# VectorE's order in the head, and the clearing of a table and the comparison of indices spread over three iterations

## The chip, the cores and the metric

The kernel runs on one core of a Trainium2 chip. The metric is the device time of one execution in microseconds; lower is better. The engines are named TensorE (PE in rows; PEld is its loading of weights), VectorE (DVE), ScalarE (ACT), GpSimd (POOL) and SyncE (SP, which issues most DMAs).

## The reference, cut to what matters

Attention with four query heads for each key head, a residual and a layer norm; then a mixture of experts whose weights are a common matrix plus sparse entries, again with a residual and a layer norm. `x` is 8 x 512 x 512, there are 16 query heads and 4 key heads of 128, 8 experts, and 4096 sparse entries for each expert.

```python
q, k, v = x @ wq, x @ wk, x @ wv            # 16 heads of q, 4 of k and v, each 128 wide
out = softmax(mask(q k^T * 128**-0.5)) v    # causal, in chunks
x = layernorm(x + out @ wo)
logits = clip(xt @ gate_w.T, -50, 50); top_w, top_idx = top_k(logits, 2)
deltas = softmax(expert_atom_weights) @ atoms            # 8 x 4096
weighted = deltas * sigmoid(importance)
rows, cols = mask_idx // H, mask_idx % H                 # 4096 places, with repeats
contrib = segment_sum((xt[:, cols] * vals).T, rows)      # vals: the two chosen experts' entries
x = layernorm(x + xt @ W.T + contrib.T)
```

## The kernel before, in words

All engines have a program of their own, written out by hand; the order of the calls in each program is the order of its work, and semaphores join them. The attention is one loop over 32 iterations `it`, eight batches `b` of four groups `g`; an iteration takes one key head and its four query heads over 512 positions. Every fp32 matrix product is made of three passes over a high and a low part of each operand (lines 1532 to 1534): ScalarE or GpSimd rounds the high part (`kT_hi`, `qT_hi`, `pT_hi`, `oT_hi`, `w_hi`), VectorE or GpSimd subtracts it (`kT_lo`, `qT_lo`, `pT_lo`, `oT_lo`, `w_lo`). Inside an iteration, `n` counts heads: `scores`, then `maxima` on VectorE (line 1922), `exps` on ScalarE, `inverse` on VectorE (`row_inv`, line 1930), `normalize` on GpSimd (`probs`, line 1409), `transposes` on TensorE (line 1559), then `pT_hi` and `pT_lo` (line 1933), then `values_first` and `values_second` on TensorE. `values_second` waits for the last `pT_lo` of the iteration, the second query projection of the next iteration waits for `kT_lo`.

**The head** stands ahead of iteration 0. Besides the first projections and scores VectorE makes there the values of the sparse entries: `importance_shares` (two steps, lines 1001 and 1002) and `make_entries` (line 1035), which multiplies them by the mixture that TensorE makes in `mix_atoms` (line 947); and it splits the value weights (`wv_lo`, line 1978), which TensorE needs from iteration 0 on.

**Iterations 0 to 3** (batch 0, no routing yet) carry three further jobs:

- The table of expert weights in HBM is first written with the common matrix. It has 16 parts, in 8 pairs. GpSimd fills a part from `wT` (`fill_part`, line 898 and 1098), SyncE stores it (`store_part`, line 908), and the two buffers are used in turn, so that part k waits for the store of part k - 2 to land. `PART_PAIRS` says which pairs go with which iteration, and position in the tuple says the place in the iteration.
- Entries whose index occurs more than once have to be summed first, and written once. The 4096 indices lie as 32 columns of 128; a quad is four columns. For a quad `equal_indices` (line 1052) compares its indices with all in their column and gives 0/1 matrices `same`; `count_later` (line 1061, four instructions) counts for each entry the equal ones that come later; TensorE multiplies `same` with the entries (`sum_entries`, line 955), and VectorE copies the sums out (`keep_sums`, lines 1071 and 1072). The indices come by a broadcast load of half of them, `load_all_indices`.
- GpSimd splits `wo` (lines 1098, 1401) and the query and key weights of later iterations (lines 1098, 769), and SyncE stores these parts to be fetched by later batches.

Of the kernel before, what the change touches and what calls it, by code (L numbers as in the profile page):

```python
# [19 lines left out]
F32 = mybir.dt.float32  # L20
# [8 lines left out]
P = 128  # L29
# [8 lines left out]
QUAD = 4  # L38
# [3 lines left out]
PART_PAIRS = ((0, 1, 2), (3, 4, 5), (6, 7))  # L42
# [754 lines left out]
class Entries:  # L797


    def __init__(self, arena, zone, same, product, rows, sem):  # L800
# [22 lines left out]
        self.s_w_in, self.s_atoms_in, self.s_all_in = sem("w_ffn_loaded"), sem("atoms_loaded"), sem("idx_rows_loaded")  # L823
# [10 lines left out]
BANK_IMP, BANK_IDX, BANK_MIX = 0, 1, 2  # L834
SMALL_LINES, SMALL_MAX, SMALL_MIXTURE, SMALL_TURNED = 1, 2, 3, 4
# [75 lines left out]
def load_all_indices(sp, N, mask_idx, half):  # L911

    rows = mask_idx.unsqueeze(0).broadcast_to([P, NS])
    sp.dma_start(N.idx_all[:].rearrange("p j n -> p (j n)"), rows[:, half * NS // 2:(half + 1) * NS // 2]).then_inc(N.s_all_in, 16)
# [36 lines left out]
def sum_entries(pe, N, psum, bank, half):  # L951

    pe.wait_ge(N.s_same, (half + 1) * QUADS // 2)
    for j in range(NJ // 2):
        last = pe.matmul(psum[:, bank, j * 2 * NE:(j + 1) * 2 * NE], N.same[:, j // QUAD, j % QUAD],
                         N.parts[:, half * NJ // 2 + j].rearrange("p s e -> p (s e)"), start=True, stop=True)
    last.then_inc(N.s_sum, 1)
# [81 lines left out]
def split_entries(dve, N):  # L1039
    dve.wait_ge(N.s_entry, 1)  # L1040
    entry_step(dve, N, dve.tensor_copy(N.parts[:, :, 0], N.entry[:]))
    entry_step(dve, N, dve.tensor_tensor(N.parts[:, :, 1], N.entry[:], N.parts[:, :, 0].bitcast(F32), ALU.subtract))


def equal_indices(dve, N, q):
# [10 lines left out]
def count_later(dve, N, upper, q):  # L1056

    at = q % (QUADS // 2)
# [7 lines left out]
def keep_sums(dve, N, psum, bank, half, entry_sum):  # L1066

    dve.wait_ge(N.s_sum, half + 1)
    sums = psum[:, bank, 0:NJ * NE].rearrange("p (j s e) -> p j s e", s=2, e=NE)
    at = slice(half * NJ // 2, (half + 1) * NJ // 2)  # L1070
# [4 lines left out]
def entry_rows(dve, R, N, row_i):  # L1075
# [7 lines left out]
    dve.wait_ge(N.s_read, 2)  # L1083
# [53 lines left out]
def attention(nc, sem, s_passed, psum, ident, causal, upper, ones, R, F, E, N, table, row_i, entry_sum, y_acc, x_rows,  # L1137
# [62 lines left out]
    def sync(sp):  # L1200
# [53 lines left out]

        def slot(j, use, g):
# [26 lines left out]
        load_all_indices(sp, N, mask_idx, 0)  # L1282
        for j in range(3):
            keep_slot(j, 1)

        def iteration(b, g, it, kind, route, job):
# [13 lines left out]
            slot(3, it + 1, after)  # L1300
            if kind == "end":
# [10 lines left out]
            if not route and g < len(PART_PAIRS):  # L1312
                for k in PART_PAIRS[g][:1]:
                    store_part(sp, N, d_dram, 2 * k)
                    store_part(sp, N, d_dram, 2 * k + 1)
# [1175 lines left out]
```

## Time and profile before

| | |
|---|---|
| median of 3 runs | 1854.17 us (1852.67 to 1855.17) |
| profiled execution | 1852.85 us, its span 1851.1 us |
| TensorE busy | 1780.5 us, 96% of the span |
| VectorE / ScalarE / GpSimd busy | 67% / 44% / 43% |
| mean granted clock of TensorE | 0.989 of 2.4 GHz |
| the chain that ended last | TensorE 81%, VectorE 6%, issue 4%, GpSimd 3%, DMA 2% |

The profile is one execution. A matrix product's end is modelled, so its busy time is not its peak rate; what counts is where TensorE is idle and for whom. The windows give busy time by stretch, the waits who ended the idle time, and the timeline single instructions. Iteration 0 takes about 30 to 78 us, iteration 1 up to 128, iteration 2 up to 178, and batch 0 ends near 234 us.

### The profile page before, as it was taken

To read this page: it belongs to the slowest core of one execution; us is meant where nothing else is said; L and a number is where in the kernel's file an instruction comes from. 1 tells how busy PE (TensorE), PEld (TensorE's weight loads), DVE (VectorE), ACT (ScalarE), POOL (GpSimd) and SP (SyncE) were. 2 spreads that over 40 slices of the span, in tenths; PEclk is the share of its full clock that TensorE was granted. 3 is DMA by queue.
4 is the path that set the end of the run, shared out by engine and by line. 5 is a ranking of instruction groups with operands and counts; after the bars stand their busy time and mean duration, and the time that the engine had idled before them with its cause. 6 is when DMAs were issued, how large, how long until landed. Compare 5 with 4: busy or idle time off the path is not lost.

```text
span 1851.1 us, 33403 instructions
## 1 busy us (share of the span) xinstructions
PE 1780.5 (96%) x9290; PEld 1503.1 (81%) x9290; DVE 1243.4 (67%) x3879; ACT 814.4 (44%) x2059; POOL 801.1 (43%) x1092
## 2 busy tenths in 40 slices
PE   8999999999999999999999999999999999999992
PEld 6788888888888888888888888888888887777772
DVE  5467567775777577757776777677766777763266
ACT  4443444443444344534544544454444443333344
POOL 6675335445444333323332333233323334666563
PEclk9999999999999999999999999999999999999996
DMA  9556353334333444454544444454445338544698
GB/s 327 197 208 221 109 205 115 115 109 145 120 116 113 155 146 153 147 170 133 164 155 173 136 149 158 155 179 152 148 137 211 114 126 308 199 160 160 229 336 315
DMA packets 157103, 317.93 MB, mean 172 GB/s; under 512 B 23056, under 2 KB 66224, under 8 KB 146160
## 3 DMA queue, kind: packets, MB, share of 16 engines
q1 hardware_dynamic: 138624, 275.83, 43.8%
q0 software_dynamic: 18288, 39.80, 6.9%
q8 instruction: 89, 1.46, 0.3%
q14 instruction: 102, 0.84, 0.1%
HBM read 227.30 MB, written 88.28 MB: 170 GB/s over the span
## 4 chain that ended last, share of the span: by engine, by line
PE 81%; DVE 6%; issue 4%; POOL 3%; DMA 2%; ACT 2%; DVEq 1%; SPq 0%; another core or an unknown queue 0%; ACTq 0%; POOLq 0%
PE psum L1532 22%; PE psum L1534 22%; PE psum L1533 21%; PE psum L1559 7%; PE psum L2298 2%; PE psum L2300 2%; PE psum L2299 2%; DMA token_rows<-x,ids_now 1%; DVE pT_lo L1933 1%; PE psum L370 1%; ACT probs L1809 1%; PE psum L792 1%; POOL probs L1409 1%; POOL expert_weights L1429 1%; POOL expert_slots L647 0%
## 5 line engine op out<-in xcount | busy, mean ns | idle before, releaser
L1409 POOL TENSOR_SCALAR probs<-probs,row_inv 128x128 f32<-128x128 f32 (+3 forms) x512 | 307.3, 624 | 428.1 <-DVE row_inv L1930 426.0
L1809 ACT ACTIVATE probs<-probs,neg_max 128x512 f32<-128x512 f32 (+3 forms) x512 | 282.5, 554 | 360.4 <-DVE neg_max L1922 358.3
L1532 PE MATMUL psum<-xT_hi,w_hi 128*128 128x512 f32 x640 | 252.9, 395 | 1.9 <-DVE kT_lo L1933 1.2
L1534 PE MATMUL psum<-xT_hi,w_lo 128*128 128x512 f32 x640 | 250.3, 391 | 0.0
L1533 PE MATMUL psum<-xT_lo,w_hi 128*128 128x512 f32 x640 | 250.0, 391 | 0.0
L1922 DVE CUSTOM_DVE_ANT_0 probs<-psum,causal 128x512 f32<-128x512 f32 (+3 forms) x512 | 223.3, 488 | 35.0 <-PE psum L1534 14.7
L1933 DVE TENSOR_TENSOR pT_lo<-psum,pT_hi 128x512 fp32r<-128x512 f32 (+1 forms) x384 | 206.5, 594 | 23.3 <-ACT pT_hi L1819 23.1
L1819 ACT CAST pT_hi<-psum 128x512 fp32r<-128x512 f32 (+1 forms) x384 | 172.4, 526 | 68.3 <-PE psum L1559 68.2
L1532 PE MATMUL psum<-wo_hi,oT_hi 128*128 128x512 f32 x496 | 196.8, 397 | 0.0
L1534 PE MATMUL psum<-wo_hi,oT_lo 128*128 128x512 f32 x496 | 194.1, 391 | 0.0
L1533 PE MATMUL psum<-wo_lo,oT_hi 128*128 128x512 f32 x496 | 193.6, 390 | 0.0
L1532 PE MATMUL psum<-kT_hi,qT_hi 128*128 128x512 f32 (+3 forms) x512 | 173.5, 339 | 0.5 <-DVE qT_lo L1947 0.5
L1559 PEld LDWEIGHTS psum<-ident,probs 128*128 128x128 f32 x1280 | 145.7, 140 | 29.9 <-DVE pT_lo L1933 11.2
L1559 PE MATMUL psum<-ident,probs 128*128 128x128 f32 x1280 | 161.5, 273 | 7.1 <-DVE pT_lo L1933 3.6
L1533 PE MATMUL psum<-kT_lo,qT_hi 128*128 128x512 f32 (+3 forms) x512 | 165.7, 324 | 0.0
L1534 PE MATMUL psum<-kT_hi,qT_lo 128*128 128x512 f32 (+3 forms) x512 | 165.1, 322 | 0.0
L1387 POOL CAST v_hi<-v_raw 128x512 fp32r<-128x512 f32 x32 | 27.4, 855 | 300.3 <-PE psum L1534 284.8
L1947 DVE SCALAR_TENSOR_TENSOR qT_lo<-psum,qT_hi 128x512 fp32r<-128x512 f32 x128 | 88.4, 690 | 96.3 <-ACT qT_hi L1823 92.2
L1823 ACT ACTIVATE qT_hi<-psum 128x512 fp32r<-128x512 f32 x128 | 76.2, 595 | 165.5 <-PE psum L1534 164.2
L1532 PE MATMUL psum<-pT_hi,v_hi 128*128 128x512 f32 (+1 forms) x384 | 140.4, 366 | 5.0 <-DVE pT_lo L1933 4.5
L1532 PEld LDWEIGHTS psum<-xT_hi,w_hi 128*128 128x128 f32 x640 | 120.5, 188 | 26.0 <-DVE kT_lo L1933 1.6
L1534 PEld LDWEIGHTS psum<-xT_hi,w_lo 128*128 128x128 f32 x640 | 120.3, 188 | 25.5
(251 smaller groups left out, 3878.1 us busy)
## 6 DMA issues: line engine op xcount, KB each, us to landing
w_hi<-split_qk_weights SPq DMA_DIRECT2D x140, 256.0 KB, 2.7
w_lo<-split_qk_weights SPq DMA_DIRECT2D x140, 256.0 KB, 3.0
wo_hi<-split_out_weights SPq DMA_DIRECT2D x27, 1024.0 KB
wo_lo<-split_out_weights SPq DMA_DIRECT2D x27, 1024.0 KB
expert_weights_hi_lo<-split_expert_weights SPq DMA_DIRECT2D x8, 2048.0 KB, 9.6
x_in<-in_L_attn_x_dram SPq DMA_DIRECT2D x8, 1024.0 KB, 7.2
expert_weights<-fill SPq DMA_DIRECT2D x16, 512.0 KB, 4.0
attn_residual<-y_acc SPq DMA_DIRECT2D x8, 1024.0 KB
```

The lines of the kernel that those rows point to most:

```text
L1409: last = pool.tensor_scalar(p, p, row_inv[:, buf, i:i + 1], 1.0, ALU.mult, ALU.mult)
L1532: pe.matmul(dst, hi_s, hi_m, start=start, stop=False)
L1533: pe.matmul(dst, hi_s, lo_m, start=False, stop=False)
L1534: return pe.matmul(dst, lo_s, hi_m, start=False, stop=stop)
L1559: last = pe.transpose(psum[:, BANKS_PT[unit], at:at + P], probs[:, buf, src:src + P], ident[:])
L1809: last = act.activation(probs[:, buf, a:a + w], probs[:, buf, a:a + w], ACT.Exp, bias=neg_max[:, buf, i:i + 1], scale=-1.0, accum_out=row_ ...
L1819: act.copy(pT_hi[:, buf, a:z], psum[:, BANKS_PT[u], 0:z - a]).then_inc(s_pt_hi, 1)
L1823: act.mul(qT_hi[:, buf], psum[:, bank, :], SCALE).then_inc(s_q_hi, 1)
L1922: last = dve.tensor_tensor_reduce(probs[:, buf, a:a + w], psum[:, BANK_S + bank, col:col + w], causal[:, T - w:T], -1.0, -MASKED, ALU.add, ...
L1933: dve.tensor_tensor(lo, src, hi.bitcast(F32), ALU.subtract).then_inc(done, 1)
L1947: dve.scalar_tensor_tensor(out=qT_lo[:, buf], in0=psum[:, bank, :], scalar=SCALE, in1=qT_hi[:, buf].bitcast(F32), op0=ALU.mult, op1=ALU.su ...
L2298: pe.matmul(dst, hi_of(j, c), hi, start=c == 0, stop=False)
```

## The change

In the head VectorE leaves the importance shares until behind the first `inverse`, and `wv_lo` until behind the first maxima. The pairs of parts go 2, 3, 3 to iterations 0, 1, 2 where they went 3, 3, 2; the place at an iteration's tail, behind the last normalization, is gone, and there is a new first place behind weight slot 3. The eight quads go 2, 3, 3 to iterations 0, 1, 2 where they went 0, 4, 4; indices are loaded in four pieces of two quads into two halves of the buffer. The sums follow with each iteration.

```diff
-PART_PAIRS = ((0, 1, 2), (3, 4, 5), (6, 7))
+PART_PAIRS = ((None, 0, 1), (2, 3, 4), (5, 6, 7))
+QUADS_OF = ((0, 1), (2, 3, 4), (5, 6, 7))
+QUAD_BUFS, LOAD_QUADS = 4, 2
@@ sum_entries
+    pe.wait_ge(N.s_same, quads[-1] + 1)
+    pe.wait_ge(N.s_chain, PARTS_MADE)
+    for k, q in enumerate(quads):
@@ equal_indices
-    at = q % (QUADS // 2)
-    if at == 0:
-        dve.wait_ge(N.s_all_in, 16 * (q // (QUADS // 2) + 1))
-        if q:
-            dve.wait_ge(N.s_sum, 1)
+    at, k = q % QUAD_BUFS, q // LOAD_QUADS
+    if q % LOAD_QUADS == 0:
+        dve.wait_ge(N.s_all_in[k % 2], 16 * (k // 2 + 1))
+    if q >= QUAD_BUFS:
+        dve.wait_ge(N.s_sum, 1 + (q - QUAD_BUFS in QUADS_OF[1]))
@@ SyncE, iteration
             slot(3, it + 1, after)
+            if not route and g < len(PART_PAIRS):
+                store_pair(PART_PAIRS[g][0])
...
             if not route and g < len(PART_PAIRS):
-                for k in PART_PAIRS[g][1:]:
-                    store_part(sp, N, d_dram, 2 * k)
-                    store_part(sp, N, d_dram, 2 * k + 1)
-            if not route and g == 1:
-                sp.wait_ge(N.s_counted, QUADS // 2)
-                load_all_indices(sp, N, mask_idx, 1)
+                store_pair(PART_PAIRS[g][2])
+            if not route and g < 2:
+                sp.wait_ge(N.s_counted, LOAD_QUADS * (g + 1))
+                load_all_indices(sp, N, mask_idx, g + 2)
@@ GpSimd, iteration
             slot(3, it + 1)
+            if not route and g < len(PART_PAIRS):
+                fill_pair(PART_PAIRS[g][0])
...
             if kind != "end":
                 normalize(n + 4, 0)
-            if not route and g < len(PART_PAIRS):
-                for k in PART_PAIRS[g][2:]:
-                    fill_pair(k)
@@ TensorE, iteration
-            elif g >= 2:
-                pe.wait_ge(N.s_read, g - 1)
+            elif g:
+                pe.wait_ge(N.s_read, g)
...
-            if not route and kind == "group":
-                sum_entries(pe, N, psum, BANKS_PT[0], g - 1)
+            if not route and g < len(QUADS_OF):
+                sum_entries(pe, N, psum, BANKS_PT[0], QUADS_OF[g])
@@ VectorE, head
-        importance_shares(dve, N)
         kT(0)
         keep_mixture(dve, N, psum)
-        dve.wait_ge(F.s_wv_hi, 1)
-        dve.tensor_tensor(wv_lo[:], wo_raw[:, 0:C, :], wv_hi[:].bitcast(F32), ALU.subtract).then_inc(s_wv, 2)
         qT(0, 0, BANK_B)
         qT(1, 1, BANK_A)
         dve.wait_ge(N.s_const, 4)
         maxima(0, 0)
+        dve.wait_ge(F.s_wv_hi, 1)
+        dve.tensor_tensor(wv_lo[:], wo_raw[:, 0:C, :], wv_hi[:].bitcast(F32), ALU.subtract).then_inc(s_wv, 2)
         inverse(0, 0)
+        importance_shares(dve, N)
         make_entries(dve, N, psum, BANK_B)
@@ VectorE, iteration (first and second quad: before and behind the inverses, as before)
             route_logits(dve, R, tt, (6,), products)
-            if quad is not None:
-                equal_indices(dve, N, quad + 2)
+            for q in quads[2:3]:
+                equal_indices(dve, N, q)
...
-            if quad is not None:
-                equal_indices(dve, N, quad + 3)
+            for q in quads[2:3]:
+                count_later(dve, N, upper, q)
             if kind in ("group", "batch"):
                 kT(it + 1)
...
-            if quad is not None:
-                count_later(dve, N, upper, quad + 2)
             if kind != "end":
                 qT(n + 4, 0, bank_of_query(0, kind))
...
-            if quad is not None:
-                count_later(dve, N, upper, quad + 3)
```

The work of VectorE in the head, where `entry` are the values of the sparse entries. Before:

```order
L1017 TENSOR_SCALAR gap_f<-row_f,spare_f 128x32
L1001 TENSOR_SCALAR entry<-entry 128x256
L1002 RECIPROCAL entry<-entry 128x256
L1933 TENSOR_TENSOR kT_lo<-psum,kT_hi 128x512
L1025 COPY eawT<-psum 64x8 x2
L1978 TENSOR_TENSOR wv_lo<-wo_raw,wv_hi 128x2048
L1947 SCALAR_TENSOR_TENSOR qT_lo<-psum,qT_hi 128x512 x2
L1922 ISA probs,neg_max<-psum,causal 128x512
```

After the change (between the two pieces stand the rest of the four maxima):

```order
L1025 TENSOR_SCALAR gap_f<-row_f,spare_f 128x32
L1948 TENSOR_TENSOR kT_lo<-psum,kT_hi 128x512
L1033 COPY eawT<-psum 64x8 x2
L1962 SCALAR_TENSOR_TENSOR qT_lo<-psum,qT_hi 128x512 x2
L1937 ISA probs,neg_max<-psum,causal 128x512
...
L1937 ISA neg_max 128x1
L1996 TENSOR_TENSOR wv_lo<-wo_raw,wv_hi 128x2048
L1945 RECIPROCAL row_inv<-row_sum 128x4
L1009 TENSOR_SCALAR entry<-entry 128x256
L1010 RECIPROCAL entry<-entry 128x256
L1043 TENSOR_TENSOR entry<-psum,entry 128x128 x2
```

`kT_lo` and the two `qT_lo` moved ahead of `wv_lo` and the two steps on `entry`.

GpSimd from the tail of iteration 0 (`v_lo`, the normalization of the next iteration's first head) into iteration 1 (the second head's normalization, then weight slot 3). Before:

```order
L1392 TENSOR_TENSOR v_lo<-v_raw,v_hi 128x512
L1409 TENSOR_SCALAR probs<-probs,row_inv 128x128
...
L1409 TENSOR_SCALAR probs<-probs,row_inv 128x512
L1098 TENSOR_SCALAR fill<-wT 128x1024 x2
L1409 TENSOR_SCALAR probs<-probs,row_inv 128x128
...
L1409 TENSOR_SCALAR probs<-probs,row_inv 128x512
L1098 TENSOR_SCALAR w_hi<-w_raw 128x512
L769 TENSOR_TENSOR w_lo<-w_raw,w_hi 128x512
```

After:

```order
L1406 TENSOR_TENSOR v_lo<-v_raw,v_hi 128x512
L1423 TENSOR_SCALAR probs<-probs,row_inv 128x128
...
L1423 TENSOR_SCALAR probs<-probs,row_inv 128x512
L1423 TENSOR_SCALAR probs<-probs,row_inv 128x128
...
L1423 TENSOR_SCALAR probs<-probs,row_inv 128x512
L1108 TENSOR_SCALAR w_hi<-w_raw 128x512
L771 TENSOR_TENSOR w_lo<-w_raw,w_hi 128x512
L1108 TENSOR_SCALAR fill<-wT 128x1024 x2
```

The fill of a pair of parts moved from between the two normalizations to behind slot 3.

VectorE in iteration 1, from `oT_lo` to the last `pT_lo`; `same` is a comparison of a quad, `equal_later` one of its four counts, and a "..." stands for the counts left out and their second instructions. Before:

```order
L1933 TENSOR_TENSOR oT_lo<-psum,oT_hi 128x2x256
L1052 TENSOR_TENSOR same<-idx_all,idx_f 128x512
L1933 TENSOR_TENSOR oT_lo<-psum,oT_hi 128x2x256
L1052 TENSOR_TENSOR same<-idx_all,idx_f 128x512
L1933 TENSOR_TENSOR kT_lo<-psum,kT_hi 128x512
L1933 TENSOR_TENSOR pT_lo<-psum,pT_hi 128x512 x2
L1933 TENSOR_TENSOR pT_lo<-psum,pT_hi 128x256
L1061 ISA equal_later,dup<-same,upper 128x128
...
L1947 SCALAR_TENSOR_TENSOR qT_lo<-psum,qT_hi 128x512
L1061 ISA equal_later,dup<-same,upper 128x128
...
L1947 SCALAR_TENSOR_TENSOR qT_lo<-psum,qT_hi 128x512
L1933 TENSOR_TENSOR pT_lo<-psum,pT_hi 128x512 x2
```

After:

```order
L1948 TENSOR_TENSOR oT_lo<-psum,oT_hi 128x2x256
L1061 TENSOR_TENSOR same<-idx_all,idx_f 128x512
L1948 TENSOR_TENSOR oT_lo<-psum,oT_hi 128x2x256
L1070 ISA equal_later,dup<-same,upper 128x128
...
L1070 ISA dup 128x1
L1948 TENSOR_TENSOR kT_lo<-psum,kT_hi 128x512
L1948 TENSOR_TENSOR pT_lo<-psum,pT_hi 128x512 x2
L1948 TENSOR_TENSOR pT_lo<-psum,pT_hi 128x256
L1962 SCALAR_TENSOR_TENSOR qT_lo<-psum,qT_hi 128x512 x2
```

Two runs of four counts went from between `pT_lo`, `qT_lo` and `qT_lo`; one run stands now ahead of `kT_lo`.

## Rows read from the trace of the kernel before

**Rows 1.** Windows: busy PE, PEld, DVE, ACT, POOL; clock, DMA share, GB/s

```profile
77.00:125.00 48.00, 43.23 (x230) 36.74 (x229) 32.12 (x97) 18.87 (x52) 34.92 (x43) 1.00 0.61 214
125.00:172.00 47.00, 44.13 (x239) 38.01 (x238) 33.35 (x98) 19.27 (x53) 30.98 (x38) 0.98 0.58 212
```

**Rows 2.** TensorE's waits from 0 to 235 us: in total, times, longest

```profile
PE psum L1532 <- DVE pT_lo L1933: 4.5, 2, 2.9
PE psum L1559 <- POOL probs L1409: 3.2, 1, 3.2
PE psum L1532 <- DVE kT_lo L1933: 1.2, 1, 1.2
PE psum L1532 <- DVE qT_lo L1947: 0.5, 1, 0.5
```

**Rows 3.** Timeline, TensorE in the head: start us, us, instruction, idle before

```profile
19.91 0.50 PE L1532 MATMUL psum<-xT_hi,w_hi 128*128 128x512 f32 x1 [1.18 <-DVE kT_lo L1933]
```

**Rows 4.** Windows with the low granted clock (columns as in rows 1)

```profile
31.00:35.00 4.00, 4.00 (x16) 3.59 (x16) 2.07 (x11) 1.04 (x3) 3.42 (x6) 0.62 1.08 403
170.00:174.00 4.00, 4.00 (x12) 3.29 (x13) 2.21 (x9) 0.59 (x1) 0.00 (x0) 0.57 0.98 293
```

**Rows 5.** Timeline, ScalarE (first row) and VectorE in the head

```profile
15.68 0.59 ACT L1827 CAST kT_hi<-psum 128x512 fp32r<-128x512 f32 x1 [3.17 <-PE psum L1534]
...
16.69 0.66 DVE L1001 TENSOR_SCALAR entry<-entry 128x256 f32<-128x256 f32 x1
17.38 1.75 DVE L1002 RECIPROCAL entry<-entry 128x256 f32<-128x256 f32 x1
...
20.14 2.38 DVE L1978 TENSOR_TENSOR wv_lo<-wo_raw,wv_hi 128x2048 fp32r<-128x2048 f32 x1
...
27.77 0.18 DVE L1930 RECIPROCAL row_inv<-row_sum 128x4 f32<-128x4 f32 x1 [1.31 <-ACT probs L1809]
30.84 0.49 DVE L1035 TENSOR_TENSOR entry<-psum,entry 128x128 f32<-128x128 f32 x2 [2.90 <-PE psum L947]
```

**Rows 6.** Chain that ended last (first row), then timeline, 82 to 100 us

```profile
82.90 7.18 DMA expert_weights<-fill
...
84.27 0.17 DVE L1930 RECIPROCAL row_inv<-row_sum 128x4 f32<-128x4 f32 x1
...
91.26 2.06 POOL L1409 TENSOR_SCALAR probs<-probs,row_inv 128x128 f32<-128x128 f32 x4
...
99.65 2.27 POOL L1409 TENSOR_SCALAR probs<-probs,row_inv 128x128 f32<-128x128 f32 x4 [4.28 <-DVE row_inv L1930]
```

**Rows 7.** Timeline, iteration 1: VectorE's comparisons beside GpSimd's splitting of weights

```profile
109.27 0.68 DVE L1052 TENSOR_TENSOR same<-idx_all,idx_f 128x512 fp32r<-128x512 int32 x1
...
112.67 1.29 POOL L1401 TENSOR_TENSOR wo_lo<-wo_raw,wo_hi 128x512 fp32r<-128x512 f32 x1 [0.18 <-POOL wo_hi L1098]
...
112.99 1.12 DVE L1061 CUSTOM_DVE_ANT_0 equal_later<-same,upper 128x128 f32<-128x128 f32 x1
...
113.88 0.39 PE L1532 MATMUL psum<-xT_hi,w_hi 128*128 128x512 f32 x1
...
116.78 0.27 DVE L1061 CUSTOM_DVE_ANT_0 equal_later<-same,upper 128x128 f32<-128x128 f32 x1
116.98 1.36 DVE L1061 CUSTOM_DVE_ANT_0 equal_later<-same,upper 128x128 f32<-128x128 f32 x1
```

**Rows 8.** First load of the indices, how loads landed, VectorE's gaps in iteration 0

```profile
28.40 1.64 SPq L914 DMA_DIRECT2D idx_all<-in_L_ffn_mask_idx_dram  x1
...
DMA to landing us min/median/max: 5.4/7.9/10.4
...
49.39 0.18 DVE L1930 RECIPROCAL row_inv<-row_sum 128x4 f32<-128x4 f32 x1 [1.33 <-ACT probs L1809]
...
52.79 0.69 DVE L1947 SCALAR_TENSOR_TENSOR qT_lo<-psum,qT_hi 128x512 fp32r<-128x512 f32 x1 [3.23 <-ACT qT_hi L1823]
```

**Rows 9.** Timeline, TensorE: one of the two groups of sums over equal indices

```profile
127.70 1.85 PE L955 MATMUL psum<-entry_hi_lo,same 128*128 128x16 f32 x16
```

More of the change, by code:

```diff
@@ L948, in mix_atoms, with sum_entries @@
     last.then_inc(N.s_mixed, 1)
[L951 to L956, printed above, removed]
+def sum_entries(pe, N, psum, bank, quads):
+    pe.wait_ge(N.s_same, quads[-1] + 1)
+    pe.wait_ge(N.s_chain, PARTS_MADE)
+    for k, q in enumerate(quads):
+        for j in range(QUAD):
+            at = (k * QUAD + j) * 2 * NE
+            last = pe.matmul(psum[:, bank, at:at + 2 * NE], N.same[:, q % QUAD_BUFS, j],
+                             N.parts[:, q * QUAD + j].rearrange("p s e -> p (s e)"), start=True, stop=True)
     last.then_inc(N.s_sum, 1)
@@ L1991, in iteration @@
             late = route and kind == "first"
-            quad = (g - 1) * QUADS // 2 if not route and kind == "group" else None
+            quads = QUADS_OF[g] if not route and g < len(QUADS_OF) else ()
             maxima(n + 1, 1)
@@ L1995, in iteration @@
                 split_entries(dve, N)
-            if not route and g >= 2:
-                keep_sums(dve, N, psum, BANKS_PT[0], g - 2, entry_sum)
+            if not route and g:
+                keep_sums(dve, N, psum, BANKS_PT[0], g - 1, entry_sum)
             if early:
@@ L2020, in iteration @@
                 route_logits(dve, R, tt, (1,), products)
-            if quad is not None:
-                equal_indices(dve, N, quad)
+            for q in quads[0:1]:
+                equal_indices(dve, N, q)
             if not route and kind == "batch":
@@ L2031, in iteration @@
                 route_logits(dve, R, tt, (2, 3), products)
-            if quad is not None:
-                count_later(dve, N, upper, quad)
+            for q in quads[0:1]:
+                count_later(dve, N, upper, q)
             if late:
@@ L2048, in iteration @@
                 route_logits(dve, R, tt, (4,) if early else (3,), products)
-            if quad is not None:
-                equal_indices(dve, N, quad + 1)
+            for q in quads[1:2]:
+                equal_indices(dve, N, q)
             inverse(n + 3, 1)
@@ L2053, in iteration @@
                 route_logits(dve, R, tt, (5,) if early else (4, 5), products)
-            if quad is not None:
-                count_later(dve, N, upper, quad + 1)
+            for q in quads[1:2]:
+                count_later(dve, N, upper, q)
             if kind == "first":
@@ L2079, in iteration @@
                 route_best(dve, R, tt)
-            if quad is not None:
-                count_later(dve, N, upper, quad + 2)
             if kind != "end":
@@ L2085, in iteration @@
                 route_chosen(dve, R, tt)
-            if quad is not None:
-                count_later(dve, N, upper, quad + 3)
             if kind != "end":
```

42 lines of the change are left out of this document (26 added, 16 removed).

## The prediction

> **What bounds the kernel now.** I read the windows first, then TensorE's waits, then the timeline ahead of each wait. TensorE is busy for 96% of the span on the page, so an edit on another engine is worth only what TensorE waits for it. The change touches the head (0 to 30 us) and iterations 0, 1 and 2, some 30 to 178 us. In the windows of iterations 1 and 2 TensorE is busy 43.2 of 48 us and 44.1 of 47 us [rows 1]: 7.6 us of gap. Its waits say for whom: 3.2 us for the `probs` that GpSimd normalizes, and 4.5 us in two pieces, the longer 2.9 us, for `pT_lo` of VectorE; besides, in the head, 1.2 us for `kT_lo` and 0.5 us for `qT_lo` [rows 2, 3]. The granted clock shows a further loss: it falls to 0.57 over the 4 us behind the wait of 2.9 us, and to 0.62 over 4 us behind the narrow products of the mixture in the head [rows 4]; full speed is 2.4 GHz and the low level 1.2 GHz.
>
> **The change, part by part.**
>
> *VectorE in the head.* ScalarE has `kT_hi` ready at 15.68 + 0.59 = 16.27 us, but VectorE takes the two steps of the importance first, from 16.69 to 19.13 us, and only then `kT_lo` [rows 5]. With them gone `kT_lo` comes 19.13 - 16.69 = 2.4 us earlier, more than the wait of 1.2 us, which goes whole. `wv_lo`, 2.38 us from 20.14 [rows 5], stood ahead of the first `qT_lo`; with it gone the wait of 0.5 us goes too. Gain 1.7 us. What is moved must fit elsewhere. VectorE was idle for 1.31 us until 27.77 and for 2.90 us until 30.84 [rows 5], so it was through with the first maxima at 26.5; 1.7 us earlier that is 24.8. Then come `wv_lo` until 27.2, the inverse, the importance with 0.66 + 1.75 = 2.4 us until 29.7, and the entries with 0.5 us until 30.2. TensorE asks for `wv_lo` behind the mixture, near 30.8 - 1.7 = 29.1 us, and for the entries only behind another set of scores, which lies in the 4 us at low clock from 31 us on [rows 4]. Cost taken: nothing, since both are there 2 us ahead. Were each of the moved steps held up by one GpSimd instruction of 1.3 us [rows 7], it would be 0 to 1 us.
>
> *The cleared table on GpSimd.* At the tail of iteration 0 a pair of parts stood ahead of the normalization that TensorE needs next. The chain that ended last runs through it: a store of the pair before takes 7.18 us, from 82.90 to 90.09, GpSimd fills behind it and normalizes only at 91.26 us, although VectorE had `row_inv` ready at 84.27 + 0.17 = 84.4 [rows 6]. With the pair behind that normalization and slot 3, `probs` are ready near 84.4 + 2.1 = 86.5 instead of 93.3 us, 6.8 us earlier against a wait of 3.2: it goes whole. Gain 3.2 us. Nothing on GpSimd is late next: the pair waits for the same store, landing at 90.1, in front of a gap of 4.28 us that ends at 99.65 [rows 6]. Bounds of its new place: 0, or one us for each by which the store lands after some 97 us. In iteration 1 the same pair made TensorE wait for nothing; moved, it gives nothing and costs nothing. On SyncE its stores now stand behind the keeping of slot 3 and ahead of that of slot 4; within the iteration nobody reads what these write.
>
> *Comparisons, 2, 3 and 3 quads instead of 0, 4 and 4.* At the end of iterations 1 and 2 VectorE counted two quads between `pT_lo`, `qT_lo` and the last `pT_lo`. Beside GpSimd's splitting of weights a count is long: that from 112.99 ends at 114.11, the GpSimd instruction from 112.67 at 113.96, and another takes 1.36 us where one of 0.27 stands ahead of it [rows 7]. So the last `pT_lo` was late and TensorE waited 4.5 us. Now no count stands there, as in iteration 0, where TensorE does not wait for `pT_lo`. Gain 4.5 us, and with the wait of 2.9 us the low clock behind it: 4 x (1 - 0.57) = 1.7 us [rows 4].
>
> Instead one quad's four counts stand ahead of `kT_lo`, from where the fourth comparison stood, 109.27 us [rows 7] (times before the shift). If short and long ones alternate they take 2 x (0.27 + 1.36) = 3.3 us, and `kT_lo` ends at 109.3 + 3.3 + 0.7 = 113.3. TensorE asks for it at 113.88, at the start of the second query [rows 7]. Bounds: four short ones, 1.1 us, end at 111.1; four long ones, 5.4 us, end at 115.4, 1.5 us late, in both iterations. I take the middle, which costs nothing, because the rows show both lengths in turn. It hides behind the first query's twelve products and has 0.6 us to spare.
>
> Iteration 0 gets two quads. The first comparison, 0.7 us, fits in the 1.33 us in which VectorE waited for the exponentials, its four counts in the 3.23 us ahead of `qT_lo` [rows 8]. The second stands ahead of `kT_lo` beside GpSimd's fill, for which no row shows a count; by the ends above it costs 0 to 1.5 us. I take 0, since short counts there leave `kT_lo` on time.
>
> *Sums on TensorE.* 32 narrow products in three groups instead of two; 16 take 1.85 us [rows 9], so the work stays and one more start costs 0 to 0.3 us. I take 0.1.
>
> **A rule weighed.** The row shows a count that ends when GpSimd's instruction ends [rows 7]. The Trainium skill, SBUF — State Buffer, section "Who interferes with whom", says that a VectorE instruction with two SBUF inputs and a GpSimd instruction that reads SBUF exclude each other, the second to issue being blocked until the first has finished. By this rule the trace agrees. It speaks against the counts' new place: by it each of the four may meet an instruction of the splitting, and the sum would be 8.0 instead of 11.0, which is rival A, worked out there from rows.
>
> **Sum.** 1.7 + 3.2 + 4.5 + 1.7 - 0.1 = 11.0 us. The profiled execution took 1852.85 us (span 1851.1, the rest lies around it); it would take 1841.9. It lies 1.3 us under the median of the runs, 1854.17, so the median becomes 1843.2. TensorE's work behind the first batch waits only for engines that are released by TensorE's own earlier work, so I carry the gain to the end.
>
> **Rivals.**
> (A) The counts are long each time: `kT_lo` 1.5 us late twice, 3.0 us. 8.0 are left, 1846.2; with a low clock behind it once, 1.7 more, 1847.9. For it: the rows of 1.12 and 1.36 us; against: the short one between them.
> (B) The low clock of the head goes too, because TensorE comes to it without two gaps: 4 x (1 - 0.62) = 1.5 us more [rows 4], 1841.7. Against it: the narrow products just ahead of it are unchanged.
> (C) The lead is not carried. A store, a load or GpSimd's splitting in iteration 1 or 2 is late in absolute time and TensorE waits for that instead, as it did behind the store of 7.18 us. It gives back what GpSimd's and VectorE's moves brought, and 1.7 us are left: 1852.5, no difference to be told. Against it: GpSimd has gaps such as that of 4.28 us [rows 6].
> (D) Slower. The first comparison now needs the indices in iteration 0. They are asked for at 28.40, and the slower of the two loads landed after 10.4 us, so at 38.8; VectorE would want them near 49.4 - 1.3 - 1.7 = 46.4 and is next awaited near 52.8 - 1.7 = 51.1 [rows 8]. From there each us of delay costs one, and the mechanism decides for slower from a landing at 62 us on. At 66 us it is 4 us slower, 1858. Only a queue held up for 25 us would do it.
>
> **How the numbers follow.** Forecast 0.60 (1843.2, by itself 1841.5 to 1845); A 0.16; B 0.09; C 0.09; D 0.03; another delay of that sign 0.03. Eight in ten: forecast, B and both times of A, with 1.3 us for the spread of the runs: 1840.0 to 1849.0. About 0.2%, 3.7 us, is what a measurement can tell from no change. Faster by more: forecast, A, B and a little of C, 0.86. Within: most of C, 0.09. Slower: 0.05.
>
> **What would show it.** Right: no wait of TensorE for `kT_lo`, `qT_lo` or `probs` up to 225 us, windows of iterations 1 and 2 full, the clock at 1.00 where it was 0.57, and batch 0 ending 11 us earlier, at 223. A new wait of 1 to 1.5 us for `kT_lo` at an iteration's end would be A; GpSimd waiting for its store with `probs` late behind it, C; VectorE waiting for `idx_all`, D. The prediction is wrong in its mechanism if TensorE waits as before although the orders have changed, or if a lead at 223 us is gone by the end.

## The result and the profile after

| | before | after |
|---|---|---|
| median, runs side by side | 1852.67 us (1848.52 to 1855.17, 5 runs) | 1840.18 us (1839.82 to 1842.5, 5 runs) |
| the same pair again, later | 1856.6 us (1853.23 to 1862.87, 11 runs) | 1844.61 us (1843.44 to 1845.79, 6 runs) |
| span of the profiled execution | 1851.1 us | 1838.2 us |

The ratio is 0.9932 with a 95% interval of 0.9918 to 0.9946, and 0.9931 (0.9917 to 0.9945) the second time: 12.5 and 12.0 us faster. Both kernels took 4 us more the second time, so a time is compared only with times taken beside it.

First TensorE's waits from 0 to 235 us of the kernel after, which answer to [rows 2] (who was waited for: us in total, times, longest):

```profile
PE psum L794 <- DMA x_in<-in_L_attn_x_dram: 7.8, 1, 7.8
```

Only the load of `x` at the very start is left. `probs`, `pT_lo`, `kT_lo` and `qT_lo` are all gone. Then its windows, which answer to [rows 1] and [rows 4] (columns as there; the third is the head's place of the low clock, the fourth lies where iteration 2 now ends):

```profile
77.00:125.00 48.00, 48.00 (x260) 41.25 (x259) 31.25 (x100) 22.00 (x61) 35.84 (x46) 1.00 0.72 253
125.00:172.00 47.00, 47.00 (x254) 40.35 (x253) 29.79 (x92) 19.59 (x53) 29.30 (x37) 1.00 0.59 220
31.00:35.00 4.00, 4.00 (x20) 3.30 (x19) 0.79 (x3) 1.84 (x7) 3.70 (x6) 1.00 1.08 397
156.00:160.00 4.00, 4.00 (x25) 3.48 (x23) 3.77 (x12) 1.57 (x4) 2.25 (x3) 1.00 0.74 299
```

TensorE is busy for all of 48 and 47 us where it was for 43.23 and 44.13, at full clock, in the head too. GpSimd's timeline from 81 to 93 us shows why `probs` are not late any more; it answers to [rows 6]:

```profile
81.30 2.06 POOL L1423 TENSOR_SCALAR probs<-probs,row_inv 128x128 f32<-128x128 f32 x4 [2.60 <-DVE row_inv L1945]
...
87.01 2.06 POOL L1108 TENSOR_SCALAR fill<-wT 128x1024 f32<-128x1024 f32 x2 [1.58 <-DMA expert_weights<-fill]
92.92 2.27 POOL L1423 TENSOR_SCALAR probs<-probs,row_inv 128x128 f32<-128x128 f32 x4 [3.84 <-DVE row_inv L1945]
```

GpSimd now waits for VectorE's `row_inv`, where `row_inv` waited for GpSimd before. The fill still waits 1.58 us for its store, but in front of a gap of 3.84 us. The shares of the chain that ended last show the same: TensorE has 84% where it had 81%, and VectorE 4% where it had 6%.

```profile
PE 84%; DVE 4%; issue 4%; DMA 3%; POOL 2%; ACT 2%; DVEq 0%; ACTq 0%; POOLq 0%; SPq 0%
```

How the lead grew, by TensorE's landmarks in the two traces (the start of a group of transposes; differences of start times):

| landmark | before | after | lead |
|---|---|---|---|
| first transposes, iteration 0 | 39.65 | 35.38 | 4.27 |
| first transposes, iteration 1 | 86.19 | 82.85 | 3.34 |
| second, behind the wait for `probs` | 93.37 | 86.70 | 6.67 |
| first transposes, iteration 3 | 186.99 | 173.28 | 13.71 |
| behind batch 0 | 240.75 | 227.04 | 13.71 |
| middle of the program | 817.41 | 804.14 | 13.27 |
| first transposes, iteration 24 | 1199.04 | 1187.17 | 11.87 |
| last transposes | 1546.71 | 1534.46 | 12.25 |
| end (span) | 1851.1 | 1838.2 | 12.9 |

The 0.93 us between the first two lines are the sums that now stand in iteration 0; they come back in iterations 1 and 2, which have fewer.

Between batch 0 and iteration 24 the lead falls by 1.84 us, and by 1.53 us in the second pair of traces. TensorE's waits in the later batches, from 235 to 1500 us, before and after:

```profile
PE psum L1559 <- DVE pT_lo L1933: 3.6, 7, 0.7
PE psum L1534 <- issue: 0.5, 1, 0.5
```

```profile
PE psum L1574 <- DVE pT_lo L1948: 4.1, 6, 0.7
PE psum L1547 <- issue: 2.2, 3, 0.8
```

Behind the last transposes 304.4 us are left before and 303.8 after; over the 13 traces of this text it is 302.4 to 310.0 us. The two traces of the kernel before are 6.3 us apart in their spans and 4.7 there, those of the changed kernel 5.8 and 6.2.

### The profile page after: what moved, and what is told of

The parts are those of the page before. It is cut to its first block, busy times and chain, and to the rows that moved or that the text cites. A ratio compares the mean times of both kernels' runs of the same rounds, so it can differ in the third digit from the quotient of the medians.

```text
span 1838.2 us, 33411 instructions
## 1 busy us (share of the span) xinstructions
PE 1776.5 (97%) x9290; PEld 1502.2 (82%) x9290; DVE 1236.2 (67%) x3881; ACT 814.6 (44%) x2059; POOL 798.7 (43%) x1092
## 4 chain that ended last, share of the span: by engine, by line
PE 84%; DVE 4%; issue 4%; DMA 3%; POOL 2%; ACT 2%; DVEq 0%; ACTq 0%; POOLq 0%; SPq 0%
PE psum L1547 23%; PE psum L1549 22%; PE psum L1548 22%; PE psum L1574 7%; PE psum L2309 2%; DMA token_rows<-x,ids_now 2%; PE psum L2311 2%; PE psum L2310 2%; PE psum L372 1%; ACT probs L1824 1%; PE psum L794 1%; DVE pT_lo L1948 1%; POOL expert_weights L1443 1%; POOL probs L1423 0%; POOL expert_slots L649 0%
```

## The experiments

Lead means here how much earlier TensorE reaches the same landmark than in the first trace of the kernel before. Four kernels ran first, together; the kernel before took 1851.94 us beside them (35 runs, 1845.17 to 1858.07).

### Each part alone

**The head.** Only VectorE's order in the head is changed:

```diff
-        importance_shares(dve, N)
         kT(0)
         keep_mixture(dve, N, psum)
-        dve.wait_ge(F.s_wv_hi, 1)
-        dve.tensor_tensor(wv_lo[:], wo_raw[:, 0:C, :], wv_hi[:].bitcast(F32), ALU.subtract).then_inc(s_wv, 2)
         qT(0, 0, BANK_B)
         qT(1, 1, BANK_A)
...
         maxima(0, 0)
+        dve.wait_ge(F.s_wv_hi, 1)
+        dve.tensor_tensor(wv_lo[:], wo_raw[:, 0:C, :], wv_hi[:].bitcast(F32), ALU.subtract).then_inc(s_wv, 2)
         inverse(0, 0)
+        importance_shares(dve, N)
```

> The kernel before with VectorE's new order in the head alone. Additive theory: the two waits for kT_lo and qT_lo go and about 2 us are kept to the end; with the low clock behind the mixture gone too, 3.5 us. Rival: the lead reaches only to iteration 1, because there the normalization on GpSimd stands behind a store to HBM that hangs on the queues' time and not on TensorE's; then the wait for probs grows from 3.2 to 5 or 7 us by as much as the head gained, and the time is that of before within 1 us.

Measured: 1848.58 us, ratio 0.9982 (0.997 to 0.9994), 3.3 us. The waits for `kT_lo` and `qT_lo` are gone; those for `probs` and `pT_lo` stand as they were, not grown (TensorE's waits up to 235 us):

```profile
PE psum L1532 <- DVE pT_lo L1933: 4.4, 2, 2.9
PE psum L1559 <- POOL probs L1409: 3.2, 1, 3.2
```

So the lead from the head, 3.2 us at the first transposes, isn't swallowed by the later waits: the engines behind them start earlier by the same lead. The waits are terms that add.

**The table.** Only the places of the pairs of parts are changed (`PART_PAIRS`, `store_pair`, `fill_pair` as in the change's diff); the quads stay 0, 4, 4.

> The kernel before with the new places of the parts of the cleared table alone. Theory: the wait of 3.2 us for probs goes and nothing takes its place, 3.2 us faster; the waits for kT_lo, qT_lo and pT_lo stay at 1.2, 0.5 and 4.5 us. Rival: GpSimd waits for the same store at the new place and delays the next normalization, 0 to 2 us faster. In the head the clock should fall again behind the mixture if that hangs on the two gaps before it.

Measured: 1847.99 us, ratio 0.9987 (0.9973 to 1.0001), too close to 1 to call it faster by the times alone. The trace is clear: no wait for `probs` is left, the lead jumps by 3.33 us at that place, and `pT_lo` (4.5, longest 2.9), `kT_lo` (1.8) and `qT_lo` (0.4) are waited for as before. The two gaps are back in the head, yet the clock did not fall behind the mixture.

**The quads.** Only the spread 2, 3, 3 with its loads and sums; the pairs stay 3, 3, 2 in their old places.

> The kernel of after with the head and the table's parts put back, so the comparisons of indices spread 2, 3, 3 alone. Theory: the two waits for pT_lo (4.5 us) go and with them the low clock behind the second (1.5 us), 6 us faster; the waits for kT_lo, qT_lo (head) and probs stay. Rival: counts ahead of kT_lo are blocked by GpSimd each time, a new wait of up to 1.5 us for kT_lo in iterations 1 and 2, 3 us faster.

Measured: 1848.17 us, ratio 0.998 (0.9966 to 0.9993), 3.7 us. The waits for `pT_lo` are gone, no wait for `kT_lo` comes at an iteration's end, and `probs` are waited for 2.8 and 0.5 us. The 6 us expected were missed. This trace drew longer stretches at the low clock than that of before, in the head (3.4 us lost against 1.7) and behind the wait for `probs` (none before); and of its lead of 2.97 us behind batch 0, 0.37 us are left at iteration 24. The table alone has 5.04 us behind batch 0 and 5.17 us there.

By the ratios the three parts give 3.3, 2.4 and 3.7 us, 9.4 in sum, against 12.6 for the whole; by the medians it is 3.4, 4.0 and 3.8 us, 11.1 in sum, against 12.5. The intervals of the parts are about 2.5 us wide to each side, so neither sum proves an interplay.

The loss behind batch 0 goes with the quads. In the seven traces with the spread 2, 3, 3 the lead falls by 1.5 to 2.7 us between batch 0 and iteration 24, whether it was 3 us or 14; in the other five, measured against the first trace of before like all, it changes by -1.3 to +0.1 us. TensorE's waits from 235 to 1500 us are 5.5 to 6.9 us in those seven and 4.1 to 4.8 us in the traces with the kernel before's quads and counts. Why spreading the quads over batch 0 costs TensorE time in later batches is open.

### Why the counts are long

The product of each count has two SBUF inputs, `same` and `upper`. Here the kernel before counts with one: `upper` and the kept product are left out, so its counts are others than the reference's.

```diff
-        last = dve.tensor_tensor_reduce(N.later[:, at * QUAD + j], N.same[:, at, j].bitcast(F32), upper[:], 1.0, 0.0, ALU.mult, ALU.add,
-                                        N.dup[:, q * QUAD + j:q * QUAD + j + 1])
+        last = dve.tensor_reduce(N.dup[:, q * QUAD + j:q * QUAD + j + 1], N.same[:, at, j].bitcast(F32), AX.X, ALU.add)
```

> The kernel before in which each count of equal later indices is a sum with one SBUF input of the same 128 elements (the product with the triangular matrix is left out), at the same places. If counts are long because their second SBUF input meets GpSimd's reads, none is longer than 0.4 us, the last pT_lo of iterations 1 and 2 comes 2 to 4 us earlier, the waits for pT_lo go and the kernel is 4 to 6 us faster. If eight counts are simply too much work between pT_lo and pT_lo, or if GpSimd blocks every VectorE instruction, durations stay above 1 us and the waits stay.

Measured: 1849.34 us, ratio 0.9982 (0.9967 to 0.9997), 2.6 us by the medians and 3.3 by the ratio, under the 4 to 6 expected. The counts of both kernels, each in the place it has in the order of before (instruction: duration in ns min/median/max, first and last start); first before, then with one input:

```profile
L1061 DVE CUSTOM_DVE_ANT_0 equal_later<-same,upper x32: 261/314/1372, 99.4 to 166.6; 128x128 f32<-128x128 f32 x32
```

```profile
L1061 DVE TENSOR_REDUCE dup<-same x32: 255/275/286, 100.5 to 162.9; 128x1 f32<-128x128 f32 x32
```

None of the 32 is longer than 0.29 us, although GpSimd splits the same weights beside them, and TensorE's waits for `pT_lo` up to 235 us are gone with nothing moved:

```profile
PE psum L1558 <- POOL probs L1408: 3.4, 1, 3.4
PE psum L1531 <- DVE kT_lo L1932: 2.3, 1, 2.3
```

It was the count's length, then, not its number or place as such, that made `pT_lo` late. The gain was there: from behind the wait for `probs` to behind batch 0 TensorE gains 5.9 us, the waits and the low clock behind them. It doesn't last to the end, since this trace has a longer wait for `kT_lo`, a second stretch at the low clock in the head, and 1.9 us less lead at the last transposes than behind batch 0.

The edit takes away the second SBUF input and the kept product at once. That a write to SBUF isn't what GpSimd holds up is shown by instructions with one input from PSUM, one from SBUF and a result in SBUF. The 384 `pT_lo` of the kernel before take 0.41 to 0.69 us, and its `kT_lo` of iteration 1 takes 0.69 us although it lies whole inside a `wo_lo` of GpSimd:

```profile
110.61 1.29 POOL L1401 TENSOR_TENSOR wo_lo<-wo_raw,wo_hi 128x512 fp32r<-128x512 f32 x1 [0.18 <-POOL wo_hi L1098]
110.86 0.69 DVE L1933 TENSOR_TENSOR kT_lo<-psum,kT_hi 128x512 fp32r<-128x512 f32 x1 [0.91 <-ACT kT_hi L1827]
```

The Trainium skill, SBUF — State Buffer, section "Who interferes with whom", says that a VectorE instruction with at most one SBUF input, outside the modes that use both ports, doesn't contend with GpSimd, and names the reduction among those that never do on trn2; the trace agrees, with 286 ns at most.

### How much room the counts have in their new place

The changed kernel, with the third quad's counts made twice ahead of `kT_lo` in iterations 1 and 2.

```diff
             for q in quads[2:3]:
+                count_again(dve, N, upper, q)
+            for q in quads[2:3]:
                 count_later(dve, N, upper, q)
             if kind in ("group", "batch"):
                 kT(it + 1)
```

> The changed kernel, in which VectorE makes the four counts of the third quad twice ahead of kT_lo, in iterations 1 and 2; the second making writes the same numbers, so the result is the reference's. How much room is behind the four counts? In the changed kernel they took 102.84 to 105.2, kT_lo ended at 105.86, and TensorE asked for it near 107.2: 1.3 us of room. Four more counts take 4 x 0.28 = 1.1 us where GpSimd doesn't read beside them, and up to 3.7 where it does (two of 0.28, one of 0.69 and one of 1.36 make 2.6). Theory of exclusive access (a count stands until GpSimd's instruction ends): 2.4 to 3.7 us more, so TensorE waits 1.1 to 2.4 us for kT_lo at the end of iteration 1 and about as much at the end of iteration 2, and the time is 2 to 5 us above the changed kernel's 1840.2, 1842 to 1845. Rival (counts are just short, the room is large): four more cost 1.1 us, no wait, 1840.

Measured: TensorE waits for `kT_lo` twice, 1.35 and 1.06 us, and its lead falls by 3 us (1845.01 us in one run; beside the changed kernel's 1843.44 to 1845.79 that can't show it). First VectorE and GpSimd of the changed kernel, iteration 1; then VectorE and TensorE with the counts made twice:

```profile
102.84 0.28 DVE L1070 CUSTOM_DVE_ANT_0 equal_later<-same,upper 128x128 f32<-128x128 f32 x1
102.85 0.74 POOL L1108 TENSOR_SCALAR wo_hi<-wo_raw 128x512 fp32r<-128x512 f32 x1
103.05 0.69 DVE L1070 CUSTOM_DVE_ANT_0 equal_later<-same,upper 128x128 f32<-128x128 f32 x1
103.67 0.28 DVE L1070 CUSTOM_DVE_ANT_0 equal_later<-same,upper 128x128 f32<-128x128 f32 x1
103.78 1.31 POOL L1415 TENSOR_TENSOR wo_lo<-wo_raw,wo_hi 128x512 fp32r<-128x512 f32 x1 [0.18 <-POOL wo_hi L1108]
103.88 1.36 DVE L1070 CUSTOM_DVE_ANT_0 equal_later<-same,upper 128x128 f32<-128x128 f32 x1
...
105.18 0.68 DVE L1948 TENSOR_TENSOR kT_lo<-psum,kT_hi 128x512 fp32r<-128x512 f32 x1
```

```profile
105.29 0.57 DVE L1070 CUSTOM_DVE_ANT_0 equal_later<-same,upper 128x128 f32<-128x128 f32 x1
105.79 0.28 DVE L1070 CUSTOM_DVE_ANT_0 equal_later<-same,upper 128x128 f32<-128x128 f32 x1
106.00 1.37 DVE L1070 CUSTOM_DVE_ANT_0 equal_later<-same,upper 128x128 f32<-128x128 f32 x1
107.30 0.68 DVE L1070 CUSTOM_DVE_ANT_0 equal_later<-same,upper 128x128 f32<-128x128 f32 x1
107.92 0.68 DVE L1958 TENSOR_TENSOR kT_lo<-psum,kT_hi 128x512 fp32r<-128x512 f32 x1
...
108.65 0.50 PE L1557 MATMUL psum<-xT_hi,w_hi 128*128 128x512 f32 x1 [1.35 <-DVE kT_lo L1958]
```

A count that begins inside a splitting instruction of GpSimd ends just behind it: that from 103.05 at 103.74, `wo_hi` at 103.59; that from 103.88 at 105.24, `wo_lo` at 105.09. Of the eight counts two have 1.36 or 1.37 us, three some 0.6 and three 0.28. Four take 2.34 us, from 102.84 to 105.18, and four more 2.74. TensorE asked at 108.65 - 1.35 = 107.3, `kT_lo` ended at 105.86: the room is 1.4 us.

### What each move in the head is worth

Two kernels put one of the moved steps back into the changed kernel: the importance ahead of `kT_lo`, and `wv_lo` ahead of the two `qT_lo`.

```diff
         index_rows(dve, N, psum)
+        importance_shares(dve, N)
         kT(0)
...
         inverse(0, 0)
-        importance_shares(dve, N)
```

> The changed kernel with the two steps of the importance put back ahead of kT_lo in VectorE's head; all else as changed. The prediction's step: 2.4 us of work ahead of kT_lo make TensorE wait 1.2 us. Theory: TensorE waits 1.2 to 1.8 us for kT_lo near 19 us, and this is the only wait that comes back; the second scores begin 1.2 to 1.8 us later than in the changed kernel, and the clock at the start comes up 0.5 us later, as in the kernel before. Rival (in the changed order kT_lo is set by ScalarE's kT_hi and the importance has room ahead of it): no wait.

> The changed kernel with wv_lo put back ahead of the two qT_lo in VectorE's head; all else as changed. The prediction's step: wv_lo of 2.38 us ahead of qT_lo makes TensorE wait 0.5 us. Theory: the wait of 0.5 us for qT_lo is back in the head, or up to 2.4 us of it, since everything ahead of it is now 1.7 to 2.1 us earlier while TensorE's other work is too; no other wait; TensorE's second scores begin 0.5 to 1 us later than in the changed kernel (27.93). Rival (qT_lo is set by ScalarE's qT_hi, which came earlier with the order): no wait, nothing lost. The total can't tell 0.5 us in one look; the waits can.

Measured: with the importance back TensorE waits 1.62 us for `kT_lo`, the first row, and with `wv_lo` back 0.27 us for `qT_lo`, the second kernel's row (timelines of TensorE in the head):

```profile
19.82 0.50 PE L1547 MATMUL psum<-xT_hi,w_hi 128*128 128x512 f32 x1 [1.62 <-DVE kT_lo L1948]
```

```profile
21.72 0.47 PE L1547 MATMUL psum<-kT_hi,qT_hi 128*128 128x512 f32 x1 [0.27 <-DVE qT_lo L1962]
```

With the importance back it waits for nothing else up to 235 us, and reaches its first transposes 3.49 us later than in the changed kernel. With `wv_lo` back, where 0.5 us of waiting or more were expected, it is 1.05 us later; of that 0.5 us are a later start (ScalarE begins `kT_hi` at 15.67 against 15.16 us). Their times, 1848.31 and 1843.20 us, are single runs, not taken side by side (the kernel before took 1858.26 beside the first, 1856.6 beside the second), and settle nothing by themselves.

The 3.49 us are more than the wait. Both traces begin `kT_hi` at 15.15 or 15.16 us, so the start isn't it. In the window from 26 to 34 us the clock is 0.79 with the importance back, 8 x 0.21 = 1.7 us lost, and 1.00 in the changed kernel. 1.62 + 1.7 = 3.3. So one edit brings back the wait and, in this one trace, the stretch at the low clock too; the expectation had only the wait.

### When the indices are needed

The first two loads of indices are issued behind weight slot 3 of iteration 0, at 40.23 us instead of 28.71, in the changed kernel:

```diff
-        load_all_indices(sp, N, mask_idx, 0)
-        load_all_indices(sp, N, mask_idx, 1)
...
             slot(3, it + 1, after)
+            if not route and g == 0:
+                load_all_indices(sp, N, mask_idx, 0)
+                load_all_indices(sp, N, mask_idx, 1)
```

> The changed kernel with SyncE issuing the first two loads of indices in iteration 0, behind weight slot 3, near 43 us, where it issued them near 28 in the head. They land 8.6 to 10.8 us later, so near 52 to 54 instead of 38. VectorE wants them near 43 (first comparison, ahead of row_inv) and TensorE asks for the first thing behind it, the probs, some us later. Theory that the loads have a margin of some 5 us and that from there each us costs one (rival D of the prediction): VectorE stands 8 to 11 us for idx_all, TensorE waits 6 to 11 us more in iteration 0, and the time is 1846 to 1851. Rival (VectorE's work behind the first comparison has slack of its own, 3 us ahead of qT_lo and more, and the delay is made up): TensorE waits under 3 us, the time is 1840 to 1843.

VectorE with the late loads, 46 to 49 us:

```profile
46.29 0.69 DVE L1061 TENSOR_TENSOR same<-idx_all,idx_f 128x512 fp32r<-128x512 int32 x1 [2.56 <-DMA idx_all<-in_L_ffn_mask_idx_dram]
46.90 0.17 DVE L1946 RECIPROCAL row_inv<-row_sum 128x4 f32<-128x4 f32 x1
...
48.47 0.69 DVE L1963 SCALAR_TENSOR_TENSOR qT_lo<-psum,qT_hi 128x512 fp32r<-128x512 f32 x1 [0.43 <-ACT qT_hi L1839]
```

The first load landed after 6 us, sooner than I expected, and VectorE stood 2.56 us for it. TensorE waited for nothing. The 2.3 us that VectorE had free ahead of `qT_lo` shrank to 0.43. So the loads have 2.56 us plus 0.4 us of room from VectorE's first need at 43.7 us, to a landing near 46.7, and the miss was in my expected landing; the slope of 1 behind that point wasn't reached.

### Is the low clock chance?

The kernel before lost 1.7 us at the low clock in the head, in each of its two traces. The first four experiments and the changed kernel showed it in some traces and not in others, so three kernels were profiled again.

> The changed kernel once more, for another profile of it and for more runs beside the kernel before. Median 1840 to 1841.5, ratio 0.992 to 0.995. What it tells: whether the head of the changed kernel is free of the stretch at the low clock (behind the mixture's narrow products, near 30 us) because of its order, or whether that comes by chance. If by order: clock 1.00 in all of 25 to 35 us again, and the span again 1838. If by chance: a stretch near 0.6 in this execution at even odds, and then the span 1.3 to 1.6 us longer.

> The kernel before with VectorE's head order alone, once more, for the low clock. So far the stretch near 30 us in the head stood in 4 of 5 profiles with the old places of table and comparisons, and in none of 5 with the new ones, though the work of the head that TensorE does is the same and this kernel has the changed kernel's order on VectorE. If it comes by chance: even odds here, and after the wait for probs too. If something of the new places keeps it away (only the index loads differ in the head): a stretch at 0.5 to 0.6 between 25 and 32 us again.

> The kernel before, once more, for the low clock: near 30 us in the head, behind the wait of 3.2 us for probs near 91 us and behind that of 2.9 us for pT_lo near 168 us. If chance decides, some other selection of the three shows it than in the first profile (head yes, probs no, pT_lo yes). If the place decides, the same selection. The waits themselves are as before within 0.3 us in either case.

The window from 26 to 34 us of six of the traces (columns as in rows 1; the clock is the third from the end). With a wait for `kT_lo` near 19 us, these are the kernel before, the same again, and the changed kernel with the importance back, in this order:

```profile
26.00:34.00 8.00, 8.00 (x55) 7.71 (x54) 1.86 (x10) 4.35 (x13) 7.03 (x9) 0.79 1.08 386
```

```profile
26.00:34.00 8.00, 8.00 (x58) 7.67 (x57) 2.92 (x14) 4.75 (x13) 7.03 (x10) 0.86 1.08 387
```

```profile
26.00:34.00 8.00, 8.00 (x52) 7.62 (x51) 3.99 (x9) 3.88 (x12) 7.24 (x6) 0.79 1.08 389
```

Without it, these are the head order alone, the same again, and the changed kernel again:

```profile
26.00:34.00 8.00, 8.00 (x40) 7.18 (x40) 5.59 (x15) 3.10 (x11) 7.06 (x10) 0.79 1.08 387
```

```profile
26.00:34.00 8.00, 8.00 (x49) 7.15 (x49) 5.48 (x17) 4.00 (x12) 7.06 (x9) 1.00 1.08 388
```

```profile
26.00:34.00 8.00, 8.00 (x49) 7.11 (x49) 5.37 (x15) 3.90 (x11) 6.82 (x10) 1.00 1.08 388
```

Over all 13 traces: of the six in which TensorE waits 1.2 to 2.3 us for `kT_lo`, five show the low clock (the table alone doesn't); of the seven without that wait, one does (the head order alone, the first time, at 0.79). So what I had set against each other, chance and order, both hold: the stretch is not certain in either order, since the same kernel shows it once and not the next time, and it goes with the wait. Were the two groups alike, a split this uneven to that side would come in about 1 of 40 draws. But the groups were formed after the traces were seen. By the loads of indices, the other difference in the head, the stretch stands in 4 of 6 traces with the old loads and 2 of 7 with the new, which could well be chance. The counts speak for the wait making the stretch likely; that it does, and how, is not shown.

The stretch varies in length too. With the quads alone it was the longest, 8 x 0.43 = 3.4 us lost:

```profile
29.00:37.00 8.00, 8.00 (x33) 7.28 (x33) 3.11 (x13) 2.92 (x10) 5.95 (x9) 0.57 1.07 397
```

In one of the six traces, that of the counts with one input, the clock also fell right behind the wait for `kT_lo`, to 0.64 over the window from 20 to 24 us.

The repeats missed what was expected elsewhere. The kernel before had the stretch in the head, behind `probs` and behind `pT_lo`, where the first time it wasn't there behind `probs`; its wait for `kT_lo` was 2.2 us, not within 0.3 of 1.2. The changed kernel was 4 us above the expected median, with the ratio as expected. Its trace had a span of 1844.0 us instead of 1838, with about the same lead behind batch 0: the 5.8 us more lie behind the last transposes, where it took 310.0 us against 303.8.

Behind the waits of about 3 us the clock is drawn too. The wait of 2.8 to 3.4 us for `probs` stood in six traces (before, head alone, quads alone, one input, and the two repeats of before and of the head) and was followed by the low clock in three; that of 2.9 us for `pT_lo` stood in five, and was followed by it in four. The same place of the head order alone, first and second time (TensorE's timeline at the transposes, then the window of the 5 us there):

```profile
90.17 2.40 PE L1559 MATMUL psum<-ident,probs 128*128 128x128 f32 x10 [3.16 <-POOL probs L1409]
```

```profile
90.00:95.00 5.00, 4.83 (x19) 4.55 (x19) 2.42 (x5) 1.68 (x4) 1.97 (x3) 0.50 0.43 141
```

```profile
88.88 1.31 PE L1559 MATMUL psum<-ident,probs 128*128 128x128 f32 x10 [3.11 <-POOL probs L1409]
```

```profile
89.00:94.00 5.00, 5.00 (x31) 4.52 (x32) 3.81 (x12) 2.90 (x8) 1.70 (x2) 1.00 0.42 133
```

Nearly equal waits, but ten transposes in 2.40 and in 1.31 us. The first time the stretch ate 2.7 us of lead, from 3.2 to 0.5; the second time the lead stayed at 4.4 to 4.5. This may be why single parts scatter more, and by their ratios are worth less than their share of the whole: a kernel with one long wait left still draws for the low clock behind it. The changed kernel has none up to 235 us. Its runs lie within 2.7 us, those of the kernel before beside them within 6.7.

## Why the prediction was right

The change gave 12.5 us (12.9 in the two traces) where 11.0 were forecast. The waits went where and as far as was said; the total is near because two misses of opposite sign partly cancel: the head gave 2.6 us more, and later batches gave 1.5 back. That 1840.18 us lies in the range is luck in part. It is below rival B's 1841.7, and the lowest time named less the spread, 1841.5 - 1.3, is 1840.2; the edge was set at 1840.0. The kernel before was lower too, 1852.67 where 1854.17 was the base; from there the forecast's 11.0 lead to 1841.7. Point by point:

- **All waits up to 235 us go: right.** No new one came, as the first experiments showed for each part apart.
- **Head, 1.7 us: too small.** TensorE's lead there was 4.27 us. The two waits are 1.65 of it, and 0.5 are an earlier start of the changed kernel's trace, which isn't the change's doing; 1.7 are the low clock of the next point. The remaining 0.4 us are there in the head order alone, repeated, as well, and I leave them open. The mis-sized term is the wait for `kT_lo` read in [rows 3]: 1.18 us was the smallest of six traces (1.2, 1.5, 1.6, 1.8, 2.2, 2.3). VectorE begins `kT_lo` at 19.1 to 19.2 us in all of them, held by the importance, while ScalarE's `kT_hi` begins anywhere from 14.48 to 15.68 us, and the profiled execution of before was the slowest. The wait is the difference of a fixed and a varying time. The prediction also has TensorE ask for `wv_lo` right behind the mixture; it asks behind the second scores, at 30.15 us in the changed kernel, where `wv_lo` was done at 26.15, so nothing hung on it.
- **Low clock of the head, taken as unchanged: wrong, mostly.** What rival B, with 0.09, named is what most traces show: the stretch is there in 1 of 7 without the wait for `kT_lo` instead of 5 of 6 with it. My argument against it, that the products just ahead are unchanged, doesn't settle it. It was worth 1.7 us in the two traces, and 1.7 to 3.4 in others. That it went in this pair is a draw in part.
- **`probs`, 3.2 us: right.** The lead grows by 3.33. The predicted moment was met too: they are ready at 81.30 + 2.06 = 83.4 us, where 86.5 less the lead of 3.3 is 83.2.
- **`pT_lo`, 4.5 us, and 1.7 for the clock behind it: right in this pair.** The lead grows from 6.67 to 13.71, of which 0.93 are sums moved; 6.1 are left against 6.2. In other executions the clock's share isn't there, or there are 1.5 to 2.7 us more behind `probs`, as in the repeated profile of before; I had put it down as certain at one place and absent at the other.
- **The gain carried to the end: mostly.** It was put at nothing lost. 13.71 us behind batch 0 are 11.87 at iteration 24 and 12.25 at the last transposes; the repeated pair goes from 15.5 to 14.0 and 14.2. Every trace with the spread quads loses 1.5 to 2.7 us on this way, a cost that the sum lacks. The ends of the spans, 12.9 and 13.4 us apart, add the scatter behind the last transposes.
- **Rival A, refuted at this room.** The counts are held up by GpSimd as the rule says, but not each for a whole instruction: four took 2.34 us where I took 3.3 and bounded them by 5.4, and four more behind them 2.74. The room was 1.4 us, where 0.6 was said; the mechanism of A is real, and shows as soon as the counts are doubled.
- **Rival C, refuted.** It left 1.7 us. And what is given back isn't its mechanism, a lead that meets something late in absolute time: the quads alone lose 2.6 us of a lead of 3, the table alone nothing of 5.
- **Rival D, not near.** In the changed kernel VectorE never waits for `idx_all`. It first wants them at 43.7 us, not 46.4, since the head is 4 us shorter instead of 1.7, and VectorE's room is used up at a landing near 46.7; what each us behind that costs wasn't measured.

## What to carry to other kernels

When one engine stands still for another at several places, the waits add up if each later step is released by the stalled engine's own work; a lead then travels, and here steps moved to places in front of another engine's gap made nobody wait. Follow the lead to the end all the same: some of it went in later batches, where nothing had been edited. Size a wait as the difference of the two times that meet in it, and ask which of them varies between executions: one trace gives one draw. Behind a gap of TensorE of about 3 us, price the low clock as a chance of 1.5 to 3 us beside the gap itself, and put instructions with two SBUF inputs where GpSimd isn't in a chain of reads, or leave them an instruction's length of room.

## What the runs showed of the hardware

- The low clock behind a wait is a draw: behind waits of 3.16 and 3.11 us the same ten transposes took 2.40 us once and 1.31 us once, and over all traces 7 of 11 waits of about 3 us had the stretch behind them.
- A VectorE instruction with two SBUF inputs waits for GpSimd's rounding, which has one input, as for its subtraction with two: a count took 0.69 us beside `wo_hi`, 1.36 beside `wo_lo`, 0.28 when it began between two such instructions. The comparison `same`, with two SBUF inputs as well, took from 0.69 up to 1.42 us in the changed kernel.
- A VectorE instruction with one input from PSUM and one from SBUF, `pT_lo`, took at most 0.69 us in all 384 cases of the kernel before, and a count with one SBUF input at most 0.29 in 32, beside the same work of GpSimd.
